# Two-layer macaron network on one core: weight stores moved beside the dense experts, and routing steps moved around both openings

## The chip, the cores and the metric

The kernel runs as one program on one core of a Trainium2 chip. The time is the device time of one execution, in microseconds (us), as the median of several runs; the profile shows one more execution. Engines are named as in the profile: PE (matrix products; PEld is its weight load), DVE (vector), ACT (scalar), POOL (GpSimd), SP (the queue that issues most transfers).

## What is computed

The input is 8 sequences of 512 tokens with 128 features. Six residual phases follow each other: an 8-expert layer (half weight), attention, the same 8-expert layer again with the same weights, a 16-expert layer, a state-space layer, and the 16-expert layer again. The change touches the first three.

```python
def _L0_ffn_ref(x, w_router, w1, b1, w2, b2):
    probs = jax.nn.softmax(xf @ w_router, axis=-1)
    topk_w, topk_idx = jax.lax.top_k(probs, 2)
    weights = jnp.sum(topk_w[..., None] * one_hot(topk_idx, 8), axis=1)
    h = jax.nn.gelu(jnp.einsum('te,ieh->tih', xf, w1) + b1)      # 128 -> 512
    out = jnp.einsum('tih,ihe->tie', h, w2) + b2                 # 512 -> 128
    return jnp.sum(out * weights[..., None], axis=1)
x = x + 0.5 * _L0_ffn_ref(_layernorm(x), ...)
x = x + _L0_attn_ref(_layernorm(x), ...)      # 16 heads of 8, softmax over 512 keys
x = x + 0.5 * _L0_ffn_ref(_layernorm(x), ...)
...
```

## The kernel before

`moe0_phase` is the 8-expert layer; it runs twice (`occ` 0 and 1). Each run has two stages.

**Opening (dense stage).** Sequence 0 goes through all D = 8 experts, whatever its routing, in rounds i = 0 to 7 of HC = 4 units c. A unit is three matmuls up (L913 to L915: a high and a low half of the split weights), a gelu on ACT (L975) and its high/low split (ACT L985, DVE L995), and, six units later, three matmuls down. `y_dve(i)` (L1023) then adds an expert's output to the residual with the weights `w_dense`; the PE's transposes L1014 of a later expert wait for it. Beside this the other seven sequences are routed: normalise (`seq_root` on POOL, `seq_xn` on ACT), transpose, router product and logits (`seq_T`, `seq_copy`, `seq_R`, `seq_logits`), the two best experts of a group of sequences (`pick_a`, `pick_b`, L529 to L550), the place of each token (`group_pos`, `group_copy`, then `place_a`, `place_b`, `place_c` on DVE, L587 to L636), and `group_send`: one indirect DMA of POOL (L649) per 128 rows and choice, which scatters tokens into the DRAM tensor `xs_rows` by expert. There are 56 such sends in opening 1, in groups of 16, 24 and 16. `pick_dense` (L560 to L571) and `weights_dense` (L660 to L671) make `w_dense`; `tables_dve` (L773 to L776) the table of which expert each block of rows has; `biases` and `bias_act` (L734, L739) their biases.

**Sparse stage.** NBLK = 18 blocks of 512 sorted rows follow (ALL = 26 rounds in all). SP loads a block (`x_load`, L1375), copies the up weights of its two experts (`take_up`, L1281) and stores its result to `ys_rows` (L1386); POOL copies the down weights (`take_down`, L1287); POOL later gathers the results (L281). The rounds begin with the PE transposes L850.

**Weights between the two runs.** In run 0, ACT and DVE split each expert's weights (`w_hi_act`, `w_lo_dve`) into `w_all`. `keep0(e)` (SP, L761) stores one expert's split weights, 1 MB, to the DRAM tensor `w_keep`; run 1 loads them back with `reload0(e)` (L768) and splits nothing.

**Attention.** Each sequence is a body of 16 steps: scores (L2225, L2293), maxima on DVE (L2233), exponentials on ACT (L2301), weighted sums (L2311), then `o_dve` (L2333, L2335), the output product (`ot_pe` L2342, `ot_act` L2348, `z_pe` L2353) and `z_dve` (L2363). Routing for the second run is placed in its later bodies by small tables; `last_body` places the end of group 2.

What sets the order: every engine executes its own list in program order. The lists are written out by the phase functions, and routing steps are hooked in at points (i, c) by `route_last_pe`, `route_last_act` and `route_last_dve`. The tables `PE_STEPS`, `ACT_STEPS` and `DVE_STEPS` name the routing steps in order, so that a wait can count to a step. On POOL, `beside` and `after_start` hold a send back until the dense stage has reached a given unit (semaphore `up_ready`). SP's list in run 0 is: weight loads of all phases, then waits for the biases and the sends, then `x_load(0)` and the sparse rounds. At the end of the last sparse round ACT's list has `weights_taken`, a wait until POOL has copied the last block's down weights.

## Time and profile before

| | |
|---|---|
| median of 3 runs | 1452.05 us (1448.83 to 1456.84) |
| profiled execution, its own time | 1456.71 us |
| span of the profiled execution | 1455.0 us |
| mean granted PE clock | 0.947 of full |
| busy PE / DVE / ACT / POOL | 1257.3 / 1114.6 / 881.6 / 509.6 us |
| opening 1 (first PE unit to first sparse transpose L850) | 35.7 to 109.6 us |
| sparse stage 1, from there to the first score of attention | 109.6 to 277.7 us |
| attention, to its last z_dve | 277.7 to 715.6 us |
| opening 2, to its first L850 | 715.6 to 778.0 us |
| sparse stage 2 and the other three phases | 778.0 to 1455.0 us |

All times are in us from the start of the span. A timeline row gives start, duration, engine, source line, operation and, in brackets, how long the engine was idle before and what released it. A row with xN joins N equal instructions in a row. A window row gives busy time of each engine in a stretch, the granted PE clock and the share of time for which the 16 DMA engines were busy.

### The profile page before, as it was taken

What the parts mean: (1) busy time and instruction counts of PE and PEld (TensorE: products, weight loads), DVE (VectorE), ACT (ScalarE), POOL (GpSimd) and SP (SyncE); (2) the same over time, 40 slices, a digit from 0 to 9 for tenths busy, and PEclk for the clock granted to TensorE, in tenths of its full rate; (3) what the DMA queues carried; (4) which work ended last, traced back from release to release, by engine and by line L of the source; (5) the groups of instructions that cost most, each with busy time, mean ns of one, the idle gap of its engine ahead of it and who ended that gap; (6) DMA issues with size and microseconds to landing.
All of it is one profiled execution on the core that took longest, in us unless ns stands there. A gap on an engine that the chain in (4) does not pass through costs nothing.

```text
span 1455.0 us, 22503 instructions
## 1 busy us (share of the span) xinstructions
PE 1257.3 (86%) x7168; PEld 794.6 (55%) x7168; DVE 1114.6 (77%) x2382; ACT 881.6 (61%) x1534; POOL 509.6 (35%) x760
## 2 busy tenths in 40 slices
PE   6767998679899889998679999889999788889998
PEld 5557988412322223222368998756666444666665
DVE  6856876689999989898366888777876753877875
ACT  5846776258888768887468777533433567333432
POOL 7771446543553433511362336524420210210100
PEclk9988999779999999999789999899999998999999
DMA  7535696422222212210343566455452010064444
GB/s 260 144 93 182 250 333 243 143 75 80 86 66 67 85 45 71 93 35 2 108 185 135 194 213 210 123 118 111 90 117 59 16 34 18 8 127 101 94 84 116
DMA packets 116528, 167.88 MB, mean 115 GB/s; under 512 B 18868, under 2 KB 63380, under 8 KB 115388
## 3 DMA queue, kind: packets, MB, share of 16 engines
q1 hardware_dynamic: 109244, 151.76, 35.4%
q0 software_dynamic: 7168, 14.69, 3.4%
q8 instruction: 58, 0.95, 0.3%
q14 instruction: 58, 0.48, 0.1%
HBM read 80.66 MB, written 45.09 MB: 86 GB/s over the span
## 4 chain that ended last, share of the span: by engine, by line
PE 51%; DVE 26%; issue 8%; ACT 8%; DMA 4%; POOL 2%; SPq 2%; DVEq 0%; ACTq 0%; POOLq 0%
PE bank L1615 6%; DVE shared L2233 6%; PE bank L2311 5%; PE pair L913 4%; PE pair L915 4%; PE pair L914 4%; PE pair L1527 3%; PE pair L1529 3%; PE pair L1528 3%; PE pair L2293 3%; PE pair L2225 3%; DVE shared L995 3%; ACT shared L2301 2%; DMA shared<-shared 2%; DVE shared L1603 1%
## 5 line engine op out<-in xcount | busy, mean ns | idle before, releaser
L2233 DVE TENSOR_REDUCE shared<-pair 128x2 f32<-128x1024 f32 x256 | 309.7, 1217 | 37.9 <-PE pair L2225 35.0
L2301 ACT ACTIVATE shared<-pair 128x1024 f32<-128x1024 f32 x256 | 260.5, 1022 | 49.7 <-PE pair L2293 48.1
L913 PE MATMUL pair<-shared 128*128 128x256 f32 (+1 forms) x704 | 231.5, 329 | 19.0 <-DMA shared<-shared 4.6
L995 DVE TENSOR_TENSOR shared<-shared 128x512 fp32r<-128x512 f32 x208 | 157.2, 764 | 95.1 <-ACT shared L985 92.3
L914 PE MATMUL pair<-shared 128*128 128x256 f32 (+1 forms) x704 | 220.6, 313 | 0.0
L915 PE MATMUL pair<-shared 128*128 128x256 f32 (+1 forms) x704 | 220.3, 313 | 0.0
L1582 ACT ACTIVATE shared<-pair 128x512 f32<-128x512 f32 x144 | 85.7, 596 | 180.6 <-PE pair L1529 180.4
L979 ACT ACTIVATE shared<-pair,shared 128x256 f32<-128x256 f32 x288 | 121.5, 476 | 62.7 <-PE pair L915 56.3
L1527 PE MATMUL pair<-shared 128*128 128x512 f32 x288 | 155.0, 538 | 4.9 <-DVE shared L1537 4.9
L913 PEld LDWEIGHTS pair<-shared 128*128 128x128 f32 x704 | 140.2, 199 | 28.7 <-issue 8.6
L1287 POOL CAST shared<-shared 128x1024 fp32r x72 | 82.9, 1152 | 176.0 <-PE pair L915 165.7
L915 PEld LDWEIGHTS pair<-shared 128*128 128x128 f32 x704 | 139.8, 199 | 6.7
L914 PEld LDWEIGHTS pair<-shared 128*128 128x128 f32 x704 | 139.6, 198 | 5.7 <-issue 0.2
L2311 PE MATMUL bank<-shared 128*9 128x512 f32 x1024 | 137.3, 609 | 4.5 <-ACT shared L2301 4.3
L649 POOL DMA_INDIRECT xs_rows<-shared,slots x112 | 118.1, 1055 | 57.1 <-issue 27.2
L281 POOL DMA_INDIRECT staged<-ys_rows,slots x112 | 116.1, 1037 | 57.4 <-ACT shared L2301 32.7
L1594 DVE TENSOR_TENSOR shared<-shared,pair 128x512 f32<-128x512 f32 x128 | 87.0, 682 | 58.7 <-ACT shared L1582 57.4
L1615 PE MATMUL bank<-shared,down_w 128*128 128x512 f32 x256 | 128.7, 594 | 0.6 <-DVE shared L1603 0.6
L2225 PE MATMUL pair<-shared 48*128 48x512 bf16 x512 | 103.1, 401 | 21.9 <-ACT shared L2301 10.7
L1529 PE MATMUL pair<-shared 128*128 128x512 f32 x288 | 116.1, 403 | 0.0
L1528 PE MATMUL pair<-shared 128*128 128x512 f32 x288 | 115.7, 402 | 0.0
L2293 PE MATMUL pair<-shared 51*128 51x512 bf16 x512 | 101.5, 394 | 5.9 <-DVE shared L2233 5.4
(379 smaller groups left out, 2178.8 us busy)
## 6 DMA issues: line engine op xcount, KB each, us to landing
shared<-shared SPq DMA_DIRECT2D x144, 256.0 KB
shared<-p_coef_rows SPq DMA_DIRECT2D x64, 512.0 KB, 8.4
shared<-xs_rows SPq DMA_DIRECT2D x36, 256.0 KB, 3.0
ys_rows<-shared SPq DMA_DIRECT2D x36, 256.0 KB, 2.4
w_keep<-shared SPq DMA_DIRECT2D x8, 1024.0 KB, 5.2
shared<-w_keep SPq DMA_DIRECT2D x16, 512.0 KB
shared<-p_q_parts SPq DMA_DIRECT2D x64, 96.0 KB, 2.3
shared<-p_k_parts SPq DMA_DIRECT2D x64, 96.0 KB, 2.4
```

Source lines behind the costliest of these rows:

```text
L913: nc.tensor.matmul(out_bank, w_hi, x_hi, start=start, stop=False)
L914: nc.tensor.matmul(out_bank, w_hi, x_lo, start=False, stop=False)
L915: return nc.tensor.matmul(out_bank, w_lo, x_hi, start=False, stop=stop)
L995: nc.vector.tensor_tensor(hl[u % RING][:], hid[u % RING][:], hh[u % RING][:], ALU.subtract).then_inc(s["dve_done"], 1)
L1527: nc.tensor.matmul(out_bank, w_hi, x_hi, start=start, stop=False)
L1528: nc.tensor.matmul(out_bank, w_hi, x_lo, start=False, stop=False)
L1529: return nc.tensor.matmul(out_bank, w_lo, x_hi, start=False, stop=stop)
L1615: nc.tensor.matmul(bank[6][:], w, h, start=(j == 0), stop=(j == IT - 1)).then_inc(s["down_done"], 1)
L2225: last = nc.tensor.matmul(pair_of("max", b, m)[:, f, :], qa[par][rows, c, i * P:(i + 1) * P], ka[par][rows, c, :], start=True, stop=True)
L2233: nc.vector.tensor_reduce(mneg[:, i, 2 * c:2 * c + 2], pair_of("max", b, m)[:], AX_X, ALU.max, negate=True).then_inc(s["mx_read"], 1)
L2301: nc.scalar.activation(probs[st % 2][:, 2 * p:2 * p + 2, :], pair_of("exp", b, 2 * st + p)[:], ACT.Exp, scale=scale).then_inc(s["exp_done" ...
L2311: last = nc.tensor.matmul(bank[6][32 * hh:32 * hh + HD + 1, :], v_all[:, b * TILES + kt, hh % 2 * (H // 2) + g * HG // 2 + hh // 2, :], pr ...
```

## The change

1. Run 0's eight `keep0` stores move on SP: from behind the block stores of sparse rounds 3 to 10 to one run of eight between the weight loads and `x_load(0)`, each waiting for its expert's `w_lo_dve`.
2. In run 0 the low halves of experts 4 to 7 (`LOW_AT`) are made later, the last at point (5, 3) where it was (4, 3).
3. Both runs: `tables_dve` moves from (3, 1) to (5, 0), the last group's `place_c` from (3, 0) to (4, 2), the biases from round 5 to round 6. Run 0: `weights_dense` moves from (3, 2) to (3, 1).
4. Run 1 alone: `pick_dense` and `weights_dense` leave the opening for the last body of attention (steps 12 and 15). The weights come there from an exponential on ACT (`odds_dense_act`, 128x32, at step 13) and four DVE operations, where a tanh and seven operations made them before. Group 2's `place_a` and `place_b` go from before the last `o_dve` to behind it, its `place_c` to point (0, 2) of the opening. The last sequence's steps come earlier: `seq_xn` ahead of the first gelu, T and its copy at (0, 1), R and the logits at (0, 3); picks at (1, 1), positions at (2, 1), `place_a` and `place_b` at (2, 2).
5. POOL: the sends of run 0's last group and of run 1's groups 2 and 3 are no longer held back; the last 12 sends of run 1's group 1 move ahead of `seq_root(7)`, into attention's end.
6. At the end of sparse stage 1, ACT's `weights_taken` and the split of k behind it move from point (ALL-1, 1) to (ALL-1, 3).

```diff
         def weights_act(occ):
+            nc.scalar.wait_ge(rs_["dve_step"], dve_at(occ, "pk3" if occ else "pkd"))
+            nc.scalar.activation(th_all[:], z_all[:], ACT.Tanh, scale=0.5).then_inc(rs_["act_step"], 1)
+        def odds_dense_act(occ):
             nc.scalar.wait_ge(rs_["dve_step"], dve_at(occ, "pkd"))
-            nc.scalar.activation(th_all[:], z_all[:], ACT.Tanh, scale=0.5).then_inc(rs_["act_step"], 1)
+            nc.scalar.activation(odds[:, 0:TILES, :], z_all[:, 0:TILES, :], ACT.Exp).then_inc(rs_["act_step"], 1)
...
             def route_last_dve(v, i, c):
-                if (i, c) == (1, 2):
+                if occ and (i, c) == (0, 2):
+                    place_c(v, occ, groups - 2)
+                if (i, c) == ((1, 1) if occ else (1, 2)):
                     pick_a(v, occ, groups - 1)
                     pick_b(v, occ, groups - 1)
-                if (i, c) == (1, 3):
+                if not occ and (i, c) == (1, 3):
                     pick_dense(v, occ)
...
-                if (i, c) == (3, 0):
+                if not occ and (i, c) == (3, 1):
+                    weights_dense(v, occ)
+                if (i, c) == (4, 2):
                     place_c(v, occ, groups - 1)
-                if (i, c) == (3, 1):
+                if (i, c) == (5, 0):
                     tables_dve(v)
-                if (i, c) == (3, 2):
-                    weights_dense(v, occ)
-
-            BIAS_AT = 5
+
+            BIAS_AT = 6
+            LOW_AT = ((0, 2), (0, 3), (2, 1), (4, 0), (4, 3), (5, 3))
...
                     xh_act(0)
+                    seq_xn(occ, B - 1)
...
-                    group_send(g, occ, 2, pace=lambda k, m: beside(g, 16 + k * 15 // 16, 0))
+                    group_send(g, occ, 2)
                 else:
                     seq_root(g, occ, B - 1)
-                    for part in range(1, 4):
-                        group_send(g, occ, 1, part, 4, lambda k, m: beside(g, (4 * (part - 1) + k) * 7 // 9, 2))
-                    group_send(g, occ, 2, pace=lambda k, m: beside(g, (12 + k) * 7 // 9, 2))
-                    group_send(g, occ, 3, pace=lambda k, m: beside(g, (28 + k) * 7 // 9, 2))
+                    group_send(g, occ, 2)
+                    group_send(g, occ, 3)
...
-                    q_.wait_ge(s["w_lo"], NE0)
+                    for e in range(NE0):
+                        q_.wait_ge(s["w_lo"], e + 1)
+                        keep0(e)
                 q_.wait_ge(s["act_step"], act_at(occ, "bias"))
...
-                    if occ == 0 and 2 < i < 3 + NE0:
-                        keep0(i - 3)
...
                 if (i, c) == (ALL - 1, 1):
                     biased_act("k", 0, 6)
+                if (i, c) == (ALL - 1, 3):
                     weights_taken(nc.scalar)
                     part1_act("k", 0)
...
+                    if routes and b == B - 1 and st == 12:
+                        pick_dense(v, routes)
+                    if routes and b == B - 1 and st == 15:
+                        weights_dense(v, routes)
...
                     group_send(g, routes, 1, 0, 4, lambda k, n: g.wait_ge(s["exp_done"], PER * b + 22 + 2 * k))
+                    for part in range(1, 4):
+                        group_send(g, routes, 1, part, 4)
...
                 o_dve(v, B - 1, GB - 1)
+                if routes is not None:
+                    place_a(v, routes, len(GROUPS[routes]) - 2)
+                    place_b(v, routes, len(GROUPS[routes]) - 2)
                 z_dve(v, B - 1)
```

SP at the end of opening 1's loads, before: `w_out` is the last weight load of the other phases, and the next row is `x_load(0)`, the first load of the sparse stage; the first store of split weights stands behind a block store in a sparse round.

```order
L380 DMA w_out<-in_L_attn_W_out 128x2x128
L1375 DMA shared<-xs_rows 128x2x256 [waits moe0_sent0,moe0_sent1,moe0_act_step,moe0_w_lo]
...
L1281 DMA shared<-shared 128x512
L1375 DMA shared<-xs_rows 128x2x256 [waits moe0_xT_ps]
L1386 DMA ys_rows<-shared 128x2x256 [waits moe0_dve_done]
L761 DMA w_keep<-shared 128x2048
```

The same places of SP now (`x_load` is L1385 and the block store L1396):

```order
L380 DMA w_out<-in_L_attn_W_out 128x2x128
L774 DMA w_keep<-shared 128x2048 [waits moe0_w_lo] x8
L1385 DMA shared<-xs_rows 128x2x256 [waits moe0_sent1,moe0_sent0,moe0_act_step]
...
L1385 DMA shared<-xs_rows 128x2x256 [waits moe0_xT_ps]
L1396 DMA ys_rows<-shared 128x2x256 [waits moe0_dve_done]
L1296 ISA [waits moe0_up_ready]
```

All eight stores now stand ahead of `x_load(0)`, and none is left between block stores.

DVE at attention's end, before: the picks of group 2 end with the scan into `summed_g`, then comes an `o_dve` pair, the first and last rows of `place_a` to `place_c` (L587 to L636, 24 operations), the last `o_dve` pair and `z_dve`.

```order
L550 SCALAR_TENSOR_TENSOR summed_g<-carry,picked_g 128x64 [waits moe0_dve_chain]
L2333 RECIPROCAL shared<-bank 128x16 [waits p1_o_tok,p1_oT_ps]
L2335 TENSOR_TENSOR shared<-bank,shared 128x4x32 [waits p1_o_chain]
L587 TENSOR_TENSOR rest_e<-pos_g,room_e 128x8 [waits moe0_act_step]
...
L636 TENSOR_TENSOR ex_all<-ex_all,ex_g 128x36 [waits moe0_dve_chain]
L2333 RECIPROCAL shared<-bank 128x16 [waits p1_o_tok,p1_oT_ps,moe0_dve_chain]
L2335 TENSOR_TENSOR shared<-bank,shared 128x4x32 [waits p1_o_chain]
L2363 TENSOR_TENSOR x_res<-bank,shared 128x512 [waits p1_x_bo,p1_z_ready]
```

The same place of DVE now:

```order
L550 SCALAR_TENSOR_TENSOR summed_g<-carry,picked_g 128x64 [waits moe0_dve_chain]
L2342 RECIPROCAL shared<-bank 128x16 [waits p1_o_tok,p1_oT_ps]
L2344 TENSOR_TENSOR shared<-bank,shared 128x4x32 [waits p1_o_chain]
L665 TENSOR_REDUCE nx_all<-odds 128x4 [waits moe0_act_step]
L666 RECIPROCAL rd_all<-nx_all 128x4 [waits moe0_dve_chain]
...
L2342 RECIPROCAL shared<-bank 128x16 [waits p1_o_tok,p1_oT_ps,moe0_dve_chain]
L2344 TENSOR_TENSOR shared<-bank,shared 128x4x32 [waits p1_o_chain]
L587 TENSOR_TENSOR rest_e<-pos_g,room_e 128x8 [waits moe0_act_step]
...
L617 CAST slots<-slot_f 128x16 [waits moe0_dve_chain]
L2372 TENSOR_TENSOR x_res<-bank,shared 128x512 [waits p1_x_bo,p1_z_ready,moe0_dve_step]
```

The last `o_dve` now has only the four operations of the dense weights ahead of it; `place_a` and `place_b` stand between it and `z_dve`, and `place_c` is gone from here.

DVE in opening 2, before the first `y_dve` (L1023; now L1036, and the split L995 is now L1008): what stood behind the last group's slots, before,

```order
L617 CAST slots<-slot_f 128x8 [waits moe0_dve_chain]
L995 TENSOR_TENSOR shared<-shared 128x512 [waits moe0_act_done,moe0_dve_step]
L626 SCALAR_TENSOR_TENSOR moved_e<-rest_e,jump_e 128x8
...
L773 TENSOR_TENSOR row_pick<-ident,iota 8x8
...
L660 TENSOR_SCALAR odds<-th_all 128x32 [waits moe0_act_step]
...
L1023 SCALAR_TENSOR_TENSOR x_res<-bank,w_dense,x_res 128x128 [waits moe0_yback]
```

and now:

```order
L617 CAST slots<-slot_f 128x8 [waits moe0_dve_chain]
L1008 TENSOR_TENSOR shared<-shared 128x512 [waits moe0_act_done,moe0_dve_step]
L1008 TENSOR_TENSOR shared<-shared 128x512 [waits moe0_act_done] x4
L1036 SCALAR_TENSOR_TENSOR x_res<-bank,w_dense,x_res 128x128 [waits moe0_yback]
L1036 SCALAR_TENSOR_TENSOR x_res<-bank,w_dense,x_res 128x128 x3
L1008 TENSOR_TENSOR shared<-shared 128x512 [waits moe0_act_done] x3
L626 SCALAR_TENSOR_TENSOR moved_e<-rest_e,jump_e 128x8
```

Between the slots and the first `y_dve` only splits are left: `place_c`, the tables and `weights_dense` are behind it or gone, and `pick_dense`, which stood further ahead, is gone too.

## Rows read from the trace of the kernel before

**Rows 1.** Timeline of PE, end of opening 1 (start, us, engine, line, operation, idle).
```profile
109.63 1.11 PE L850 MATMUL bank<-ident,shared 128*128 128x128 f32 x4 [8.78 <-DMA shared<-xs_rows]
```
**Rows 2.** Opening 1's sends, one line's summary (ns min/median/max, first and last start).
```profile
L649 POOL DMA_INDIRECT xs_rows<-shared,slots x56: 955/962/1933, 27.1 to 104.5; - x56
```
**Rows 3.** Timeline of SP, opening 1.
```profile
76.44 0.58 SPq L380 DMA_DIRECT2D w_out<-in_L_attn_W_out  x1
106.82 0.37 SPq L1375 DMA_DIRECT2D shared<-xs_rows  x1
```
**Rows 4.** Windows of opening 1, sparse 1, opening 2 (PE, PEld, DVE, ACT, POOL).
```profile
77.00:105.00 28.00, 23.69 (x104) 19.01 (x104) 15.90 (x34) 17.93 (x31) 22.10 (x20) 0.91 0.19 61
160.00:200.00 40.00, 37.18 (x306) 35.96 (x305) 32.85 (x51) 30.82 (x73) 16.01 (x15) 1.00 0.85 311
724.00:742.00 18.00, 16.05 (x55) 12.37 (x55) 7.76 (x21) 13.81 (x27) 14.04 (x14) 0.72 0.99 398
```
**Rows 5.** The stores of split weights, one line's summary.
```profile
L761 SPq DMA_DIRECT2D w_keep<-shared x8: 467/468/566, 170.9 to 226.2; - x8
...
DMA to landing us min/median/max: 4.7/5.2/6.1
```
**Rows 6.** Timeline of PE: blocks 8 and 17 of sparse 1, then of sparse 2.
```profile
166.80 0.60 PE L850 MATMUL bank<-ident,shared 128*128 128x128 f32 x4
...
237.84 0.60 PE L850 MATMUL bank<-ident,shared 128*128 128x128 f32 x4
...
835.44 0.60 PE L850 MATMUL bank<-ident,shared 128*128 128x128 f32 x4
...
903.89 0.60 PE L850 MATMUL bank<-ident,shared 128*128 128x128 f32 x4
```
**Rows 7.** Waits of PEld, 118 to 246 (line, waited for: us, times, longest).
```profile
PEld pair L913 <- DMA shared<-shared: 6.3, 8, 1.1
PEld bank L1014 <- issue: 3.8, 3, 3.3
```
**Rows 8.** Waits of PEld, 780 to 910.
```profile
PEld bank L1014 <- issue: 6.6, 3, 3.3
```
**Rows 9.** Timeline of ACT, end of sparse 1.
```profile
260.32 0.62 ACT L1939 CAST shared<-shared 128x512 bf16<-128x512 f32 x1 [5.83 <-POOL shared L1287]
```
**Rows 10.** Timeline of PE, end of sparse 1 and attention's first scores.
```profile
263.02 0.55 PE L913 MATMUL pair<-shared 128*128 128x256 f32 x1 [3.96 <-ACT shared L1006]
...
277.74 1.04 PE L2225 MATMUL pair<-shared 48*128 48x512 bf16 x4 [3.82 <-DMA shared<-p_k_parts]
```
**Rows 11.** Timeline of DVE, end of attention.
```profile
696.60 0.22 DVE L529 TENSOR_REDUCE mx_g<-z_all 128x8 f32<-128x64 f32 x1 [5.36 <-ACT z_all L501]
...
704.09 0.17 DVE L587 TENSOR_TENSOR rest_e<-pos_g,room_e 128x8 f32<-128x8 f32 x1 [2.49 <-ACT pos_g L517]
...
710.24 0.26 DVE L2333 RECIPROCAL shared<-bank 128x16 f32<-128x16 f32 x1
```
**Rows 12.** Timeline of PE, end of attention and opening 2.
```profile
710.97 1.09 PE L2342 MATMUL bank<-ident,shared 128*128 128x128 f32 x4 [4.49 <-DVE shared L2335]
...
730.00 1.39 PE L496 MATMUL bank<-wr,xnT 128*128 128x8 f32 x8 [1.95 <-ACT xnT L491]
...
759.34 1.09 PE L1014 MATMUL bank<-ident,shared 128*128 128x128 f32 x4 [5.63 <-DVE x_res L1023]
...
765.14 1.30 PE L734 MATMUL bank<-shared 8*128 8x36 f32 x10
...
778.01 0.66 PE L850 MATMUL bank<-ident,shared 128*128 128x128 f32 x4 [0.76 <-DMA shared<-xs_rows]
```
**Rows 13.** Windows of opening 2 (columns as in rows 4).
```profile
730.60:737.40 6.80, 6.80 (x20) 5.45 (x20) 2.07 (x3) 3.56 (x8) 5.28 (x6) 0.50 1.02 416
759.34:764.70 5.36, 5.36 (x15) 4.39 (x16) 1.74 (x3) 1.59 (x3) 1.12 (x2) 0.50 0.05 15
```
**Rows 14.** Timeline of ACT, opening 2: the biases.
```profile
770.44 0.31 ACT L739 COPY shared<-bank 128x180 f32<-128x180 f32 x1
```

More of the change, by code:

```diff
@@ L394, in build @@
         ACT_STEPS = ("xn1 xn2 c1 c2 xn3 l1 l2 xn4 c3 xn5 c4 l3 p0 xn6 c5 l4 xn7 c6 l5 xn0 c7 l6 c0 l7 p1 l0 p2 th bias".split(),
-                     "xn0 c0 l0 xn1 c1 l1 xn2 c2 l2 p0 xn3 c3 l3 xn4 c4 l4 xn5 c5 l5 p1 xn6 c6 l6 p2 xn7 c7 l7 p3 th bias".split())
+                     "xn0 c0 l0 xn1 c1 l1 xn2 c2 l2 p0 xn3 c3 l3 xn4 c4 l4 xn5 c5 l5 p1 xn6 c6 l6 od p2 xn7 c7 l7 p3 th bias".split())
         DVE_STEPS = ("st1 st2 st3 st4 st5 st6 st7 st0 pk0 sl0 pk1 sl1 pk2 pkd sl2 tables onehot".split(),
-                     "st0 st1 st2 pk0 sl0 st3 st4 st5 pk1 st6 sl1 pk2 sl2 st7 pk3 pkd sl3 tables onehot".split())
+                     "st0 st1 st2 pk0 sl0 st3 st4 st5 pk1 st6 sl1 pkd pk2 sl2 st7 pk3 sl3 tables onehot".split())
         POOL_STEPS = tuple([f"{k}{b}" for b in ORDER[occ] for k in ("var", "rs", "sh")] for occ in range(2))
@@ L668, in weights_dense @@
             ts = slice(0, TILES)
-            chain = odds_of(v, occ, ts)
+            chain = sum_odds(v, occ) if occ else odds_of(v, occ, ts)
             chain(nc.vector.scalar_tensor_tensor(out=w_dense[:], in0=odds[:, ts, :], scalar=0.5, in1=both_d[:], op0=ALU.mult, op1=ALU.mult))
@@ L1036, in route_last_pe @@
             def route_last_pe(i, c):
-                if occ and (i, c) == (0, 3):
+                if occ and (i, c) == (0, 1):
                     t_ = nc.tensor
@@ L1040, in route_last_pe @@
                     seq_T(occ, B - 1, bank[6])
-                if occ and (i, c) == (1, 0):
+                if occ and (i, c) == (0, 3):
                     seq_R(occ, B - 1, bank[6])
-                if (i, c) == (2, 3):
+                if (i, c) == ((2, 1) if occ else (2, 3)):
                     group_pos(occ, groups - 1, bank[6])
             def route_last_act(i, c):
-                if occ and (i, c) == (0, 0):
-                    seq_xn(occ, B - 1)
+                if occ and (i, c) == (0, 1):
+                    seq_copy(occ, B - 1, bank[6])
                 if occ and (i, c) == (0, 3):
-                    seq_copy(occ, B - 1, bank[6])
-                if occ and (i, c) == (1, 1):
                     seq_logits(occ, B - 1, bank[6])
-                if (i, c) == (2, 3):
+                if (i, c) == ((2, 1) if occ else (2, 3)):
                     group_copy(occ, groups - 1, bank[6])
@@ L1239, in vector @@
                         if not occ:
-                            if (i, c) in ((0, 2), (0, 3), (1, 3), (2, 3), (3, 3), (4, 3)):
-                                w_lo_dve(v, 2 + ((0, 2), (0, 3), (1, 3), (2, 3), (3, 3), (4, 3)).index((i, c)))
+                            if (i, c) in LOW_AT:
+                                w_lo_dve(v, 2 + LOW_AT.index((i, c)))
                         if c == 3 and i > 2:
@@ L1296, in after_start @@
                 if k > 3:
-                    beside(g, 1 + (k - 4) * 15 // 20, 0)
-            def beside(g, k, ahead):
-                if k > ahead:
-                    g.wait_ge(s["up_ready"], U0 + min(k - ahead, HC * D))
+                    g.wait_ge(s["up_ready"], U0 + 1 + (k - 4) * 15 // 20)
             GATHERS = {NSUB - 14 + (3 * k) // 2: (1 + k // TILES, k % TILES) for k in range(2 * TILES)}
@@ L2161, in attn_phase @@
             PLACED_IN = {4: (0, PLACE_EARLY), 7: (1, PLACE_LATE)}
-            last_body = {"pick_a": (0, 13), "pick_b": (0, 14), "pos": (0, 15), "place_a": (0, 15), "place_b": (0, 15), "place_c": (0, 15)}
+            last_body = {"pick_a": (0, 13), "pick_b": (0, 14), "pos": (0, 15)}
             GROUP_STEPS = ((3, late), (6, late), (7, last_body))
@@ L2462, in act_b @@
                             seq_logits(routes, b - 1, bank[7])
+                        if last_ and st == 13:
+                            odds_dense_act(routes)
                     if b + AHEAD < B:
```

9 lines of the change are left out of this document (8 added, 1 removed).

## The prediction

> **What bounds the kernel now.** I read the timeline of each engine around the places that the diff names, then the waits of PEld in both sparse stages, then windows for clock and transfers; no total over the kernel says what a move inside one stage is worth. Five places matter.
>
> Opening 1 is bound by POOL. Its 56 sends run from 27.1 to 104.5 without a long gap: 55 distances in 77.4 us are 1.41 each, for a median send of 0.96 [rows 2]. SP loads the first sorted block only when the last send has landed, at 106.82 [rows 3], and PE stands idle for 8.78 until 109.63 [rows 1]. What PE gains before that is lost again there.
>
> Sparse 1 is bound in part by transfers. Between 160 and 200 the 16 DMA engines are busy 0.85 of the time [rows 4]; the eight 1 MB stores go out between 170.9 and 226.2, each 4.7 to 6.1 to land [rows 5], and PEld waits 6.3 in all, eight times, for copied up weights [rows 7].
>
> The end of sparse 1: ACT waits 5.83 for POOL's last weight copy before it splits k [rows 9], with the last round's activations queued behind; PE waits 3.96 for one of these [rows 10].
>
> The end of attention: PE waits 4.49 for the last o_dve [rows 12], which stands on DVE behind place_a to place_c, 704.09 to 710.24 [rows 11].
>
> Opening 2: PE waits 5.63 for the first y_dve and 1.95 for the last sequence's transposed rows [rows 12]. After each it runs at half clock, 6.8 and 5.36 us long [rows 13].
>
> **The change part by part.**
>
> Stores into opening 1. SP's last weight load is issued at 76.44 and its next instruction at 106.82 [rows 3], a gap of 30.4. Eight stores at 0.47 are 3.7 of issue, and even at their landing times beside sparse traffic, 8 x 4.7 to 6.1 = 38 to 49 one after another, they would overlap two deep as they do now. The engines are only 0.19 busy here [rows 4], so I expect 8 MB to pass at the 398 GB/s of the full stretch of rows 4, in 21 us: from 77 to 98, ahead of the last send. The late low half of expert 7, point (5, 3), costs a wait only if it comes after about 95; the dense rounds take 5.4 each (worked out below) and y_dve(0) is due near 77, so (5, 3) lies near 85 to 90. Sends beside full engines: in 724 to 742 the share is 0.99 and POOL is 14.04 busy in 18 with 14 operations, 1.0 each [rows 4], so a send does not stretch there. The sends of group 2 lose their hold, but a hold shows nowhere in the 1.41. The routing moves of run 0 free DVE before y_dve(0); POOL's end covers that. If POOL's cover were gone, they would be worth a PE wait like opening 2's. Term: **0**, bounds -0.5 (sends a little closer) and +5 (one store's landing, rows 5, behind which x_load(0) waits).
>
> Stores out of sparse 1. Blocks 8 to 17 begin at 166.80 and 237.84, 71.0 for nine rounds; the same rounds of sparse 2, without stores, take 903.89 - 835.44 = 68.45 [rows 6]. That is 2.6, and the lower bound. But sparse 2 has 2.8 more of a stall that has no releaser in the trace (6.6 against 3.8, [rows 7, 8]), so like for like it is 5.4; the waits for weights, 6.3, give the upper bound. Term: **-5.5**, between -2.6 and -6.3.
>
> ACT's wait at the end of sparse 1. Two points later, the last round's activations no longer stand behind it. PE's 3.96 is what can go; the k split itself comes no earlier, since POOL's copy ends it, and the first scores wait 3.82 for k's parts [rows 10], so some of it may stop there. Term: **-3.5**, bounds -1.5 (a good third of PE's wait) and -5 (most of ACT's 5.83).
>
> End of attention. The last o_dve now starts when its input is there. Of PE's 4.49, o_dve itself is 0.73 (710.24 to 710.97), so 3.76 goes [rows 11, 12]. place_a and place_b, 16 of the 24 operations, then run beside ot_pe, ot_act and z_pe, some 4 us in which DVE has nothing else. pick_dense, twelve operations of about 0.22, goes into DVE's idle 5.36 before 696.60 [rows 11]. The new exponential stands on ACT between attention's own: no more than the 0.31 of a wider copy [rows 14]. If the cover of pick_dense were gone it would cost its 2.7. Twelve sends now stand ahead of seq_root(7) on POOL, 12 x 1.41 = 17 us after about 700; root may come 1 to 3 later than the residual allows, and seq_xn, now ahead of the first gelu, with it. I charge that to opening 2. Term: **-3.5**, bounds -3 and -4.5.
>
> Opening 2. Off DVE's list ahead of y_dve(0) go pick_dense, the last place_c, the tables and weights_dense: 12 + 8 + 4 + 7 operations, about 0.2 to 0.25 each, 7 us; group 2's place_c, 2.2, comes in at (0, 2), where DVE is busy 7.76 in 18 [rows 4]. So the 5.63 goes. The clock: it shows 0.50 from 759.34 to 764.70, right after that idle time; at full clock these 5.36 are 2.7 shorter. Of the 1.95 for the transposed rows I take 1.5, since seq_root(7) comes later. Against this stands a new wait. The biases end on PE at 766.44 and are copied by 770.75, 4.3 later [rows 12, 14]; from x_load(0)'s issue to PE's transposes it took 2.8 in opening 1 [rows 1, 3]; together 7.1. Before, PE had seven units in between, 778.01 - 0.76 - 766.44 = 10.8; with the biases one round later it has three, 4.6. PE waits 2.5 where it waited 0.76: +1.7. Term: -5.6 - 2.7 - 1.5 + 1.7 = **-8.1**. Upper bound -4 (no clock, no 1.5); lower -11.5 (the half-clock stretch 730.60 to 737.40 goes as well, 3.4). I leave that one out: its cause, a cold start after the long wait for weights, is only partly touched.
>
> The Trainium skill (TensorE: Matmul & The Clock Gate, "Part 1: The HAM clock gate") says that the slow clock is the default and activity lifts it. By that rule closing both waits would keep the clock up in both stretches and the sum would be 3.4 lower, about 1428. The trace agrees that half clock follows each idle stretch; no run here shows that it stays away.
>
> **Sum.** 0 - 5.5 - 3.5 - 3.5 - 8.1 = -20.6. The profiled execution's own time is 1456.71, so its like would take 1436.1. The runs shown have their median 4.7 lower, at 1452.05: **1431.5**. Their spread is near 0.5%, 7.3 us, about what a measurement can tell from no change.
>
> **The rivals.**
>
> *The stores slow the sends (slower).* Both use the same 16 engines, and opening 1 hangs on POOL. Some 20 sends are left at 77. If each had to let a store's 5.2 pass [rows 5], eight of them would cost 8 x 3.8 = 30 more: 1452 - 20.6 + 30 = 1462. It decides from 20.6 us lost, 1.0 per remaining send. At the longest send of rows 2, 1.93, the loss is about 20, and the kernel is the same. Against it: the 1.0 per operation beside full engines. Slower 0.05, about even 0.06.
 No row here shows sends beside stores.
>
> *Sparse 1 gains only 2.6*, as rows 6 say taken bare, and the tail only 1.5 because k's parts bind: 1452 - 15.7 = 1436. Chance 0.13.
>
> *Opening 2 gives little.* The clock stays half and the bias wait grows by a round, -1 in place of -8.1: 1438 to 1439; with the former together, 1443. Chance 0.10.
>
> *Full clock through opening 2.* PE reaches the transposed rows without a pause and both half-clock stretches go, 3.4 more: 1428. For it: half clock began within 1 us of the 1.95 wait's end. Against it: PE is at half clock from the long wait for reloaded weights on, which stays. Chance 0.15; it is what the rule named above says.
>
> *The change doesn't do what it says*: the last store waits for a late low half and holds x_load(0) back by 5 to 10, or attention's end is held by something behind o_dve; together with a poor opening 2 it leaves less than 7 saved, about 1446. Chance 0.06.
>
> **How the numbers follow.** The forecast (1429 to 1436) has 0.45. Below 1444.8 is "faster by over 0.5%": 0.45 + 0.15 + 0.13 + 0.10 = 0.83, and a little of the fourth, 0.84. Within 0.5%: 0.06 + 0.05 = 0.11. Slower: 0.05. The range: all terms at their good bounds give 1452 - 27.8 = 1424, and unforeseen clock gains a few more; at their bad ends without the +5 they save 11.1, 1441. I set 1422 to 1443.
>
> **What would show it.** Right: no weight-load wait for copied up weights in sparse 1 and its nine rounds near 65; the last o_dve directly behind its transposes; no wait before the first L1014 of opening 2 and full clock behind it; the last send of opening 1 still near 104 to 106; a wait of 2 to 3 before the first block's transposes in opening 2. Wrong: sends of more than 1.4 beside the stores, x_load(0) later than 108, or a new wait behind seq_root(7) at the start of opening 2.

## The result and the profile after

The median fell from 1454.07 us (4 runs, the three of the table above and a fourth of 1456.08) to 1433.68 us (4 runs, 1430.25 to 1441.01); the ratio is 0.9871, 95% interval 0.9821 to 0.992. A second series of the same kernel gave 1433.58 and 0.9886 (0.9844 to 0.9927). The forecast was 1431.5, with a range of 1422 to 1443. The profiled execution took 1434.69, its span is 1432.9.

The stages, read from one profile each, in us. The run e2, described below, is the kernel before with the stores alone moved, so outside opening 1 and sparse 1 its code is that of before; "after again" is a second profile of the changed kernel:

| stage | before | e2 | after | after again | forecast |
|---|---|---|---|---|---|
| opening 1, first dense matmul to first sparse transposes | 70.27 | 69.94 | 70.29 | 68.99 | 0 |
| sparse 1, block 0 to 8 | 57.17 | 57.12 | 57.45 | 57.36 | |
| sparse 1, block 8 to 17 | 71.03 | 66.53 | 65.56 | 66.29 | -5.5 |
| block 17 to the first score | 39.90 | 40.32 | 38.89 | 37.67 | -3.5 |
| attention up to the seventh z_dve | 398.71 | 398.64 | 399.40 | 398.95 | |
| seventh to last z_dve | 38.46 | 38.46 | 35.25 | 35.04 | -3.5 |
| last z_dve to first dense matmul | 6.07 | 6.09 | 6.10 | 6.19 | |
| opening 2, first dense matmul to first sparse transposes | 57.03 | 55.06 | 47.25 | 47.31 | -8.1 |
| sparse 2, block 0 to 17 | 125.88 | 125.25 | 126.87 | 127.01 | |
| from there to the end | 551.06 | 548.62 | 546.72 | 544.90 | |

The rows without a forecast hold the same instructions in the same order, or nearly; they show how far two executions differ. Over the thirteen profiles of this study the last row lies between 544.9 and 551.1 and attention up to the seventh z_dve between 397.2 and 404.2, so a few us there prove nothing. Two profiles of the same code can differ in a forecast row too: opening 2 is the same code in before and in e2, and they are 2.0 apart.

**Opening 1.** PE's timeline, the summary of the sends' line, that of the stores, the timeline of SP and two windows (columns as in rows 4):

```profile
109.46 1.12 PE L863 MATMUL bank<-ident,shared 128*128 128x128 f32 x4 [12.29 <-DMA shared<-xs_rows]
```
```profile
L649 POOL DMA_INDIRECT xs_rows<-shared,slots x56: 954/959/2410, 26.9 to 104.6; - x56
```
```profile
L774 SPq DMA_DIRECT2D w_keep<-shared x8: 327/1118/1321, 77.2 to 87.5; - x8
...
DMA to landing us min/median/max: 5.4/12.3/17.1
```
```profile
77.22 10.65 SPq L774 DMA_DIRECT2D w_keep<-shared  x8
106.91 0.38 SPq L1385 DMA_DIRECT2D shared<-xs_rows  x1
```
```profile
77.00:105.00 28.00, 18.43 (x89) 14.41 (x87) 17.02 (x41) 16.26 (x29) 21.91 (x21) 0.90 0.94 357
160.00:200.00 40.00, 38.12 (x318) 37.26 (x317) 34.22 (x55) 31.76 (x76) 15.99 (x15) 1.00 0.62 218
```

The last send starts at 104.6 as in [rows 2], and x_load(0) at 106.91 as in [rows 3]: the eight stores beside the sends cost nothing. POOL spends 1.04 per send in that window (21.91 for 21), where it spent 1.10 [rows 4]. The transfer engines went from 0.19 to 0.94 busy. The stores were slower than I had them: SP's issues stretch to 1.1 each in the median, a store lands up to 17.1 after its issue, and the last packet of a store in the trace ends at 103.2, not 98. That is 3.7 before x_load(0) goes. PE is done with the dense work earlier and waits 12.29 instead of 8.78 [rows 1]: what it gained is lost again to the sends, as said. The gain comes from the routing moves, since e1, which has them and no stores here, waits 12.53, and e2, which has the stores and not them, 8.65.

**Sparse 1.** PE's timeline, blocks 8 and 17:

```profile
166.91 0.60 PE L863 MATMUL bank<-ident,shared 128*128 128x128 f32 x4
...
232.47 0.60 PE L863 MATMUL bank<-ident,shared 128*128 128x128 f32 x4
```

65.56 for nine rounds, where [rows 6] gave 71.0. The waits for copied up weights of [rows 7] are gone from the list of this profile (the second one has two, 1.0 in all), and the window 160 to 200 shows the transfer engines 0.62 busy, where they were 0.85 [rows 4].

**The end of sparse 1.** Timelines of ACT, POOL, SP and PE:

```profile
257.25 0.62 ACT L1947 CAST shared<-shared 128x512 bf16<-128x512 f32 x1 [3.00 <-POOL shared L1302]
```
```profile
260.25 1.21 POOL L1972 TENSOR_TENSOR shared<-shared 128x512 bf16<-128x512 f32 x1
```
```profile
261.49 1.55 SPq L1996 DMA_DIRECT2D p_q_parts<-shared  x3
```
```profile
240.19 2.04 PE L1878 MATMUL bank<-xnT,wq_p 128*128 128x512 f32 x2 [2.82 <-issue]
...
257.37 0.35 PE L926 MATMUL pair<-shared 128*128 128x256 f32 x1 [0.25 <-POOL shared L1302]
...
271.37 1.03 PE L2234 MATMUL pair<-shared 48*128 48x512 bf16 x4 [4.72 <-DMA shared<-p_k_parts]
```

PE's 3.96 [rows 10] is down to 0.25. But SP sends q's parts only at 261.49, right when POOL's split of q ends (260.25 + 1.21), and the first score waits 4.72 for the loads behind that. In this execution PE also ran at half clock from about 239 (L1878 takes 2.04; it was 1.10 in the second profile). So the stage as a whole mixes the move with the clock; the experiment e3 takes them apart.

**Attention's end and opening 2.** Timelines of DVE and PE, and two windows:

```profile
701.29 0.26 DVE L2342 RECIPROCAL shared<-bank 128x16 f32<-128x16 f32 x1 [4.61 <-PE bank L2332]
```
```profile
702.02 1.09 PE L2351 MATMUL bank<-ident,shared 128*128 128x128 f32 x4 [0.82 <-DVE shared L2344]
...
712.11 0.76 PE L926 MATMUL pair<-shared 128*128 128x512 f32 x1 [4.23 <-DMA shared<-w_keep]
...
727.24 0.19 PE L508 MATMUL bank<-summed_g,ones_b 128*128 128x32 bf16 x1 [1.46 <-DVE summed_g L550]
...
740.36 0.60 PE L1027 MATMUL bank<-ident,shared 128*128 128x128 f32 x4
...
747.64 0.63 PE L1027 MATMUL bank<-ident,shared 128*128 128x128 f32 x4 [1.12 <-ACT shared L1015]
...
751.00 1.30 PE L747 MATMUL bank<-shared 8*128 8x36 f32 x10
...
759.36 0.66 PE L863 MATMUL bank<-ident,shared 128*128 128x128 f32 x4 [2.26 <-DMA shared<-xs_rows]
```
```profile
712.11:717.30 5.19, 5.19 (x14) 4.18 (x15) 0.40 (x1) 4.74 (x10) 3.98 (x4) 0.50 1.00 387
717.30:759.36 42.06, 37.22 (x179) 29.57 (x177) 30.18 (x88) 33.78 (x62) 21.70 (x20) 1.00 0.43 170
```

The last o_dve now waits 4.61 for PE, and PE waits 0.82 for it where it waited 4.49. In opening 2 both waits of [rows 12], 1.95 and 5.63, are gone: the transposes behind y_dve(0), at 740.36, wait for nothing. Three smaller waits stand in the list, 1.46, 1.12 and 2.26, the last one for the block that comes behind the biases. From 717.30 on the granted clock is 1.00 to the end of the stage, so both half-clock stretches of [rows 13] are gone too. Not all that this pair of profiles shows is the change. In e2, with the code of before, the half-clock stretch behind the wait for the transposed rows is 3.4 long where it was 6.8, and the stage is 2.0 shorter (window of e2, columns as in rows 4):

```profile
726.70:730.05 3.35, 3.35 (x9) 2.62 (x9) 1.35 (x2) 1.89 (x5) 2.44 (x4) 0.50 1.03 417
```

So opening 2 fell by 9.8 against before and by 7.8 against e2.

### The profile page after: what moved, and what is told of

Same layout as the page of the kernel before. It is cut to its first block and busy times, and to the rows that moved or that the text cites. A ratio compares the mean times of both kernels' runs of the same rounds, so it can differ in the third digit from the quotient of the medians.

```text
span 1432.9 us, 22499 instructions
## 1 busy us (share of the span) xinstructions
PE 1247.0 (87%) x7168; PEld 790.0 (55%) x7168; DVE 1116.8 (78%) x2379; ACT 881.4 (62%) x1535; POOL 510.8 (36%) x760
## 5 line engine op out<-in xcount | busy, mean ns | idle before, releaser
L926 PE MATMUL pair<-shared 128*128 128x256 f32 (+1 forms) x704 | 227.9, 324 | 9.9 <-DMA shared<-w_keep 4.2
L928 PE MATMUL pair<-shared 128*128 128x256 f32 (+1 forms) x704 | 218.4, 310 | 0.0
L927 PE MATMUL pair<-shared 128*128 128x256 f32 (+1 forms) x704 | 218.0, 310 | 0.0
L1008 DVE TENSOR_TENSOR shared<-shared 128x512 fp32r<-128x512 f32 x208 | 160.6, 782 | 72.8 <-ACT shared L998 69.7
L1535 PE MATMUL pair<-shared 128*128 128x512 f32 x288 | 153.7, 534 | 5.1 <-DVE shared L1545 5.1
L926 PEld LDWEIGHTS pair<-shared 128*128 128x128 f32 x704 | 138.9, 197 | 17.1 <-issue 9.0
L928 PEld LDWEIGHTS pair<-shared 128*128 128x128 f32 x704 | 138.2, 196 | 6.1
L927 PEld LDWEIGHTS pair<-shared 128*128 128x128 f32 x704 | 138.3, 197 | 5.2 <-issue 0.2
L281 POOL DMA_INDIRECT staged<-ys_rows,slots x112 | 116.9, 1044 | 58.4 <-ACT shared L2310 32.9
L1537 PE MATMUL pair<-shared 128*128 128x512 f32 x288 | 114.7, 398 | 0.0
L1536 PE MATMUL pair<-shared 128*128 128x512 f32 x288 | 114.3, 397 | 0.0
## 6 DMA issues: line engine op xcount, KB each, us to landing
w_keep<-shared SPq DMA_DIRECT2D x8, 1024.0 KB, 12.3
```

What stands on the lines that cost most here:

```text
L926: nc.tensor.matmul(out_bank, w_hi, x_hi, start=start, stop=False)
L927: nc.tensor.matmul(out_bank, w_hi, x_lo, start=False, stop=False)
L928: return nc.tensor.matmul(out_bank, w_lo, x_hi, start=False, stop=stop)
L1008: nc.vector.tensor_tensor(hl[u % RING][:], hid[u % RING][:], hh[u % RING][:], ALU.subtract).then_inc(s["dve_done"], 1)
L1535: nc.tensor.matmul(out_bank, w_hi, x_hi, start=start, stop=False)
L1536: nc.tensor.matmul(out_bank, w_hi, x_lo, start=False, stop=False)
```

## The experiments

The runs e1 to e10 each edit the changed kernel, except e2, which edits the kernel before. e3 to e8 ran once each. Their times, 1427.1 to 1435.5, lie inside the spread of the changed kernel's ten runs (1430.3 to 1442.0) or at most 3.1 below it, so only their stages and waits are read.

**Which part gave sparse 1 its 5.5?** Two runs: the changed kernel with the stores put back (e1), and the kernel before with the stores alone moved (e2).

```diff
 e1, on the changed kernel (e2: the same lines the other way round, on the kernel before)
-                    for e in range(NE0):
-                        q_.wait_ge(s["w_lo"], e + 1)
-                        keep0(e)
+                    q_.wait_ge(s["w_lo"], NE0)
...
+                    if occ == 0 and 2 < i < 3 + NE0:
+                        keep0(i - 3)
```

> The changed kernel with the eight stores of split weights put back behind the block stores of sparse rounds 3 to 10. Theory (stores compete with the copied up weights): blocks 8 to 17 of sparse 1 take 71 us instead of 65.6, with six to eight PEld waits for copied weights of 6 us in all; the rest stays, so the whole is 5.4 above the changed kernel, near 1439. Rival (the rounds are bound by DVE and ACT anyway, and the gain of 5.4 was a stall or a clock stretch that fell elsewhere): they take 66 to 68, and the whole is at most 2.6 above. Opening 1's last send starts near 104.6 in both.

> The kernel before with only the eight stores moved ahead of the first sorted block's load. Theory: blocks 8 to 17 take about 65.6 instead of 71.0, the last send of opening 1 still starts near 104.5 and the first sparse transpose at 109.6, so the whole is 5.4 shorter: 0.9963 of before. Rival (the routing moves of opening 1 or the removed hold on the sends are what keeps the sends on time beside the stores): the last send later than 106 and less than 3 gained.

Waits of PEld, 118 to 246, of e1, and the blocks 8 and 17 of e1:

```profile
PEld pair L926 <- DMA shared<-shared: 7.3, 9, 1.1
```
```profile
169.35 0.60 PE L863 MATMUL bank<-ident,shared 128*128 128x128 f32 x4
...
240.63 0.60 PE L863 MATMUL bank<-ident,shared 128*128 128x128 f32 x4
```

e1 takes 71.3 for the nine rounds, with nine waits for copied weights, and e2 66.5 with a single one of 0.9. Over all profiles the nine rounds take 71.0 and 71.3 with the stores in them, and 65.6 to 66.7, mean 66.1, in the eleven without: the stores cost 5.1. e1's ratio is 0.9917 (0.9884 to 0.995), e2's 0.997 (0.9948 to 0.9993), by that ratio 4.4 us below before. e2's sends:

```profile
L649 POOL DMA_INDIRECT xs_rows<-shared,slots x56: 954/959/1930, 27.3 to 104.5; - x56
```

So neither the routing moves nor the removed hold are needed for the stores to fit beside the sends. The theory holds from both sides. The stores do not stretch a send either: e1, without them, has a send of 2.02 at 79.5, and the changed kernel has one of 2.02 at 79.3.

The bare 2.6 of the comparison with sparse 2 was the wrong measure: a stall fell into sparse 2's rounds 8 to 17 that these rounds of sparse 1 don't have. It is 3.0 to 3.1 long and stands there in all thirteen profiles; in that of before (waits of PEld, 835.44 to 903.89):

```profile
PEld bank L1014 <- issue: 3.1, 1, 3.1
```

**ACT's wait at the end of sparse 1** (e3).

```diff
                 if (i, c) == (ALL - 1, 1):
                     biased_act("k", 0, 6)
-                if (i, c) == (ALL - 1, 3):
                     weights_taken(nc.scalar)
```

> The changed kernel with ACT's wait for POOL's last weight copy put back to point (ALL-1, 1). Theory (the move removed PE's wait of 4 us, but POOL's split of q, four operations behind its last copy, then ends last, so that only part of it came through): PE's wait in front of the last up matmuls returns with 4 us; from block 17's transposes to the first score it takes 40 to 42 us where the changed kernel took 38.9. Rival (the move does nothing, since q's split and the block stores ended last before too): 38.5 to 39.2.

Timeline of PE of e3:

```profile
255.96 0.55 PE L926 MATMUL pair<-shared 128*128 128x256 f32 x1 [3.96 <-ACT shared L1019]
...
270.57 1.03 PE L2233 MATMUL pair<-shared 48*128 48x512 bf16 x4 [3.56 <-DMA shared<-p_k_parts]
```

PE's wait returns to the hundredth, yet the stage takes 38.78, within the rival's band and 0.1 from the first profile of the changed kernel. The half clock near 239 fell into the one and not into the other, so the stage as a whole can't decide it. An event that both orders share can: POOL's last weight copy. Timelines of POOL, before, e3 and the changed kernel:

```profile
259.25 1.04 POOL L1287 CAST shared<-shared 128x1024 fp32r x1 [0.39 <-PE pair L915]
```
```profile
252.18 1.04 POOL L1302 CAST shared<-shared 128x1024 fp32r x1 [0.39 <-PE pair L928]
```
```profile
255.71 1.51 POOL L1302 CAST shared<-shared 128x1024 fp32r x1 [0.39 <-PE pair L928]
```

From block 17 to the start of that copy it takes 20.4 to 21.9 in the three profiles with the wait in its old place and 20.2 to 23.3 in the ten with the new one: this part varies, and the move doesn't shorten it. From the copy's start to the first score it takes 18.5 in before, 18.4 in e2 and e3, and 15.6 to 15.8 in all ten with the new place. So the move is worth 2.7: less than 3.5, and not nothing. From the copy's end on it is 3.2; the copy itself takes 1.5 with the wait in its new place and 1.0 in the old one, for a reason that no run here shows.

**place_a and place_b at attention's end** (e4).

```diff
-                o_dve(v, B - 1, GB - 1)
                 if routes is not None:
                     place_a(v, routes, len(GROUPS[routes]) - 2)
                     place_b(v, routes, len(GROUPS[routes]) - 2)
+                o_dve(v, B - 1, GB - 1)
                 z_dve(v, B - 1)
```

> The changed kernel with group 2's place_a and place_b put back ahead of the last o_dve; place_c stays in opening 2. Theory (o_dve waits behind what stands ahead of it on DVE): the last o_dve starts 16 operations, 3.9 us less the idle 2 to 2.5 that they may use ahead of it, later; PE's wait before ot_pe grows from 0.8 to between 2.3 and 2.9, z_dve comes 1.5 to 2.1 later. The 24 operations of the kernel before cost 3.7, so a third of the gain belongs to place_c. Rival (place_a and place_b fit whole into DVE's idle time before the last o_dve): no later than 0.3.

```profile
702.62 0.63 PE L2351 MATMUL bank<-ident,shared 128*128 128x128 f32 x4 [2.42 <-DVE shared L2344]
```

PE's timeline shows a wait of 2.42, inside the theory's 2.3 to 2.9. From the seventh z_dve to the last it takes 35.92, against 34.5 to 35.3 in the other runs with the new order, so z_dve comes 0.7 to 1.4 later, less than the 1.5 to 2.1 expected. By PE's wait the 16 operations cost 1.6 (2.42 for 0.82), and the kernel before, with place_c's eight behind them, waits 2.1 more (4.49 for 2.42). So more than half of the gain belongs to place_c, not the third that I expected: DVE's idle time ahead of the last o_dve can hide part of the first sixteen, but not the eight behind them.

**What holds opening 2** (e5, e7, e8) **and the start of sparse 1** (e6).

```diff
 e5
-                if (i, c) == (4, 2):
+                if (i, c) == (4, 0):
                     place_c(v, occ, groups - 1)
-                if (i, c) == (5, 0):
+                if (i, c) == (4, 1):
                     tables_dve(v)
-            BIAS_AT = 6
+            BIAS_AT = 5
 e6
                 x_load(0)
+                x_load(1)
                 for h in range(2):
                     at = expert(h)
                     for k in range(2):
                         take_up(q_, h, k, at)
-                x_load(1)
                 x_load(2)
 e7
-                if (i, c) == (4, 2):
+                if (i, c) == (3, 0):
                     place_c(v, occ, groups - 1)
-                if (i, c) == (5, 0):
+                if (i, c) == (3, 1):
                     tables_dve(v)
 e8: the POOL lines of the change, all undone
```

> The changed kernel with the biases back in round 5, the last place_c at (4, 0) and the tables at (4, 1). Theory (in opening 2 the first sorted block now waits for the biases, not for sends, whose last starts 10 us earlier): PE's wait of 2.3 before the first sparse transposes goes to under 0.3, and from the first dense matmul to those transposes it takes 45.0 to 45.5 where the changed kernel took 47.3. Rival (the tables, 12 operations behind, come too late for the biases in round 5, and PE waits there instead): 46.5 to 47.5. Opening 1 ends with its sends as before.

> The changed kernel with SP issuing the second sorted block's load directly behind the first one's, ahead of the four copies of up weights. Theory (PE's second wait of 4.9 at the start of sparse 1 is that load standing behind 3.8 of copies on SP): the wait shrinks to 1 to 2, and block 0 to block 8 of sparse 1 takes 53.5 to 55 where it took 57.5. Rival (the copied up weights, now later, or the high and low halves of block 0 end last): not below 57.

> The changed kernel with the last place_c and the tables put back to (3, 0) and (3, 1), ahead of the first y_dve: 12 operations, 3.1 us. Theory (DVE's list ahead of the first y_dve is what opening 2 hung on, and the changed kernel has no more than 0.3 to spare there): PE waits 2 to 3 in front of the transposes behind y_dve(0), and from the first dense matmul to the first sparse transposes it takes 48.5 to 51 where it took 47.3, more when the clock falls. Rival (taking pick_dense and weights_dense out, 4.4 us, was enough, and later waits of DVE for ACT absorb these 3.1): 47 to 47.8.

> The changed kernel with all of POOL's edits undone: sends held back as before, and group 1's last 12 sends in opening 2 behind seq_root(7). Theory (the biases end last in opening 2, with 10 us to spare for the sends): without the edits 36 sends at 1.27 follow seq_root(7) from about 710, the last near 756, and x_load(0) 1 to 3 later than with them; from the first dense matmul to the first sparse transposes 48 to 50.5. Opening 1 unchanged. Rival (the sends never bound opening 2): 47 to 47.5, and POOL's edits are worth nothing here.

PE's timelines of e5, e6, e7 and e8, in this order:

```profile
745.17 1.30 PE L747 MATMUL bank<-shared 8*128 8x36 f32 x10 [0.61 <-DVE shared L789]
...
757.11 0.60 PE L863 MATMUL bank<-ident,shared 128*128 128x128 f32 x4
```
```profile
108.61 1.12 PE L863 MATMUL bank<-ident,shared 128*128 128x128 f32 x4 [11.33 <-DMA shared<-xs_rows]
111.22 1.09 PE L863 MATMUL bank<-ident,shared 128*128 128x128 f32 x4 [1.49 <-DVE shared L876]
```
```profile
745.69 0.63 PE L1027 MATMUL bank<-ident,shared 128*128 128x128 f32 x4 [2.09 <-DVE x_res L1036]
```
```profile
760.28 1.11 PE L863 MATMUL bank<-ident,shared 128*128 128x128 f32 x4 [6.86 <-DMA shared<-xs_rows]
```

e5: the wait before the first block is gone, a wait of 0.61 for the tables takes its place, and the stage takes 44.2 instead of 47.3: a little more gain than forecast, since the 1.12 before L1027 went as well. The theory holds: in opening 2 the biases, not the sends, ended last, and putting them off to round 6 was the part of the change that cost.

e6: 53.98 from block 0 to 8 for 57.45, as the theory said. The wait of 4.94 in the changed kernel (the second load was issued at 112.17, behind 3.84 of copies) is 1.49 and now for DVE. In the two later versions with this edit, e9 and e10, the same blocks took 55.81 and 56.93. The seven profiles without this edit and without stores in sparse 1's rounds, from the changed kernel to e8, lie between 57.2 and 60.6, mean 58.4, so over all it is worth about 3.

e7: PE waits 2.09 behind y_dve(0) and the stage takes 48.5. That is the theory's lower edge; the clock did not fall. So the first y_dve had next to no time to spare, and taking out pick_dense and weights_dense alone would have left some 2 of the wait. e7 moves the two pieces in opening 1 as well, and that stage took 72.76, 2.5 longer than in the first profile: two of its sends took 1.95 and 3.07, the last send starts at 107.0 and x_load(0) goes at 109.28. So sends can stretch with the order of the routing steps; what stretched these, no run here shows.

e8: the last send starts at 755.3, x_load(0) goes at 757.57, and PE waits 6.86 where it waited 2.26; the stage takes 51.9, 1.4 beyond the theory's band. The sign is clear: POOL's edits are worth 4.6 here. I had given them no term of their own; in the kernel before, the sends still ended last in opening 2 (the last started at 773.1, x_load(0) went at 775.4, the same 2.3 later as in opening 1), so with DVE's chain gone and the sends as they were, the sends would have been the bound. The hold itself costs nothing in e8, where POOL idles at most 0.31 between two of these sends; they are late because 36 of them, not 24, follow seq_root(7).

**Two profiles of one program, and two further versions** (after_again, e9, e10). e9 joins e5 and e6; e10 also puts opening 2's positions to (2, 2) and place_a and place_b to (2, 3).

> The changed kernel again, unedited, as the measure of what differs between two profiles of one program, and beside the two versions of the same call. Theory: its median is 0.985 to 0.990 of before; the stages stand as in its first profile within 1 us each up to attention, and within 3 in attention and behind sparse 2, whose instructions are those of before: the 4.3 that its first profile was shorter there is the spread of executions. Rival: the 4.3 come back in full, and belong to the change.

> The changed kernel with two edits together: biases back in round 5 with the last place_c at (4, 0) and the tables at (4, 1), and the second sorted block's load directly behind the first. Theory: the two act in different stages and add, 3 and 3.5, so it is 6.5 below the changed kernel, near 1427 and 0.983 of before. Rival: the time saved at the start of sparse 1 or of sparse 2 is lost behind it (in the next stall of these rounds), and it is less than 3 below.

> The version before with one more edit: in opening 2 the positions of the last group at (2, 2) and its place_a and place_b at (2, 3), one unit later. Theory (PE's new wait of 1.5 before the position product is for the picks on DVE, which a unit more hides): the wait goes, and the stage from the first dense matmul to the first sparse transposes takes 42.8 to 43.5 where the biases in round 5 gave 44.2. Rival (the slots then come later and y_dve(0) with them): PE waits as long there, 44 to 45.

| kernel | median (us) | ratio to before | opening 2 | sparse 1, block 0 to 8 |
|---|---|---|---|---|
| changed, again | 1433.58 | 0.9886 (0.9844 to 0.9927) | 47.31 | 57.36 |
| e9 | 1427.98 | 0.9848 (0.9807 to 0.989) | 44.25 | 55.81 |
| e10 | 1428.31 | 0.9841 (0.9802 to 0.988) | 44.76 | 56.93 |

The changed kernel's stages repeat within 0.7 up to sparse 1's end, except 1.3 in opening 1 and 1.2 at the end of sparse 1 (the half clock there); the stretch behind sparse 2 is again shorter than before, 544.9, so its theory "spread alone" is not proven by this run. But other runs with the same code there took 549.1 (e1, e4), and the kernel before 551.1 and, as e2, 548.6. Whether one or two us of it belong to the change stays open; no instruction there was moved. e9 is 5.6 below the changed kernel by the medians, near the forecast 6.5, though the intervals overlap. The stages show the part of opening 2 in full (44.2 to 44.8 in e5, e9 and e10 for 47.3) and the part of sparse 1 only to 1.6 and 0.4 against this profile of the changed kernel.

In e10 the wait before the position product is gone as the theory said, and none is left behind y_dve(0), so the rival's cause didn't occur; yet the stage takes 44.76. Timeline of PE and a window of e10:

```profile
740.61 1.30 PE L747 MATMUL bank<-shared 8*128 8x36 f32 x10 [0.76 <-DVE shared L789]
```
```profile
742.00:745.30 3.30, 3.30 (x8) 2.55 (x9) 1.23 (x4) 1.19 (x2) 1.33 (x2) 0.50 0.13 42
```

The wait for the tables, 0.76, is hardly longer than e9's 0.62. But behind it PE ran at half clock for 3.3, which e9 did not; at full clock these are 1.65 shorter, and the stage would take 43.1, as forecast. Whether the edit or chance brought the half clock, one profile can't tell, and by the medians e10 is no better than e9.

## Why the prediction was right, point by point

The time lies in the range, and the mechanism of each forecast part showed itself. The sum was -20.6 and the five stages give -19.5 in the first pair of profiles (0.0 - 5.5 - 1.0 - 3.2 - 9.8) and -21.4 with the second profile; the ratio of the runs gives 1454.07 x 0.0129 = 18.8. That the sum came so near is in part luck: the terms missed by up to 2.5 either way, and one edit, below, had no price. The step "0" for opening 1 held, with a cover thinner than thought: the stores ended at 103, not 98, since all transfers together moved 357 GB/s here rather than 398. Two of its readings don't bear on that but are off: before, the stores did not "overlap two deep", as they went out 7.2 to 8.8 apart and landed in 4.7 to 6.1; and the 5.4 per dense round is worked out nowhere, while its own seven units in 10.8 give 6.2. The late low half was in time all the same, as the last store went out at 87.5.

The step of sparse 1, -5.5, was right, with 5.1 over all profiles, and so was the choice against the bare 2.6 (e1, e2, and the stall that only sparse 2's rounds have).

The step for the end of sparse 1, -3.5, was somewhat large: 2.7 from the start of POOL's last copy on (e3), where 0.5 is lost to a longer copy. The prediction named the reason ("some of it may stop there") but took PE's wait nearly in full. In the changed kernel POOL's split of q behind its last weight copy is the late piece: q's parts go out the moment it ends. The rest of what the first pair of profiles shows as -1.0 is the clock ahead of that copy.

Attention's end, -3.5, measured -3.2. The o_dve went as far as its input allowed; what the prediction called 1 to 3 of delay for seq_root(7) came (POOL's sends ended at 709.7; seq_root(7) starts 3.7 behind the start of the last z_dve, where it starts 2.2 behind it in e8), and PE's start was still set by the reload of weights, which it reaches as late as before.

Opening 2, -8.1, measured -9.8 against before and -7.8 against e2: the terms that were counted came (5.6, 2.7, and 1.95 for 1.5; the wait behind the biases cost 1.5 for 1.7), and others that I had not counted came on both sides. The half-clock stretch that I left out, 3.4, went as well, so in the clock the case named "full clock through opening 2" is what happened, though not in its time of 1428. Against it stand PE's new waits of 1.46 for the last group's picks and of 1.12 for ACT. With them 5.6 + 1.95 + 2.7 + 3.4 - 1.5 - 1.5 - 1.1 = 9.6. Of the 3.4 some 1.7 is the one execution that was profiled: in e2 that stretch is half as long.

What the prediction did not see is that POOL's edits carry part of this term. It priced them at nothing and took the sends to be out of the way; with those edits undone, 4.6 of the gain is gone (e8). The sum holds only because the edits were in the change.

That the slow clock is the default and activity lifts it, as the Trainium skill says (TensorE: Matmul & The Clock Gate, "Part 1: The HAM clock gate"), agrees with these profiles: full clock for 42 us in opening 2, without an idle stretch of more than 2.3. I had weighed the rule against the trace of before and taken the other case; my ground, that PE is at half clock from the long wait for weights on, holds only up to 727 of that trace, which grants full clock from 727.5 to 730.3, around the 1.95 wait. It is an agreement, not a proof, as no run put the 1.95 alone back, and an idle stretch alone doesn't tell: the clock fell behind 1.95 in before and 2.32 in e2, and did not behind 2.09 in e7.

The rivals: sends slowed by stores did not occur (e2 has the same last send as before). The rule of turns between queues in the Trainium skill (DMA: Bandwidth & Descriptors, "Queues, rings and completion order") fits that: sends went on at 0.96 while eight stores were under way, which landed up to 17.1 after their issue. A gain of only 2.6 in sparse 1: excluded by e1 and e2. Little from opening 2: excluded by the stage, 47.3 for 55.1 and 57.0. A last store held up by its low half: x_load(0) goes at 106.91, not 5 to 10 late. The new wait behind the biases came at its forecast size, and e5 shows that the change could have done without it.

## What to carry to other kernels

A queue that is idle while another engine sets the end of a stage is room for transfers of a busy stage: look at which stage has the free share, and whether the last of them ends before the stage does. Take out the chain ahead of the first result that the matrix engine needs, then ask what comes second: here removing DVE's chain would have been worth about half had POOL's last twelve sends of group 1 stayed behind seq_root(7) (e8), and the biases, put off for DVE's sake, then ended last (e5). Compare single stages of several profiles before believing a difference of 2 us; the matrix engine's clock alone moves a stage by that. Where it does, measure from an event that both orders share, as from POOL's last copy here.

## What the runs showed that I had not expected

A half-clock stretch falls into one execution of the same instructions and not into another: at the end of sparse 1 L1878's two matmuls took 2.04 in one profile and 1.10 in the next, after the same idle of 2.8. Eight stores of 1 MB queued at once beside small scattered sends slow their own issue (0.47 to 1.1 each on SP) and landing (5.2 to 12.3), while a send's 0.96 on POOL stays.
